# Row attention: the exponential in two instructions by score bank, each with its own sum and signal

## The chip, the cores and the metric

The kernel runs on one core of one Trainium2 chip. The metric is the device time of one execution in microseconds (us), lower is better. The kernel before took 1969.8 us, the median of three runs (1965.45 to 1972.23).

## The reference

A graph network with four residual blocks over 1250 rows of 512 features: a graph attention over edges, a small mixture with low-rank experts, an edge-mean network and, last, a transformer block. The change touches only the attention of that last block. Cut to what matters there:

```
q = (x @ Wq + bq).reshape(B, S, NH, dh)          # B = 1, S = 1250, NH = 8, dh = 64
k = (x @ Wk + bk).reshape(B, S, NH, dh)
v = (x @ Wv + bv).reshape(B, S, NH, dh)
scores = einsum('bqhd,bkhd->bhqk', q, k) / sqrt(dh)
attn = softmax(scores, axis=-1)                  # over all 1250 keys
ctx = einsum('bhqk,bkhd->bqhd', attn, v).reshape(B, S, D)
x = layernorm(x + ctx @ Wo + bo, g1, beta1)      # then a top-1 mixture of 8 experts, a second norm
```

Everything is float32. Where a product needs full precision, both sides are split into a high and a low part and multiplied in three passes.

## The kernel before

All parts of the network follow each other in one program. The stage at issue is `self_attention`, which fills the time from about 1381 us to 1820 us of the profiled span. Each engine has an instruction stream written out by hand; they meet only through semaphores, and no scheduler reorders anything.

**Tiling.** The 1250 queries are cut into 5 chunks of 250, each of two tiles of 125 queries. With 8 heads this gives 16 units a chunk, numbered n = 0 to 15 (head n // 2, tile n % 2), and 80 units in all. One unit is a block of 125 queries by 1250 keys. The text calls it a row of the stage, or a unit.

**One unit, in the order of its data:**

1. `scores(n)` on TensorE, L2812: six matmuls into three PSUM banks (columns 0 to 512, 512 to 1024, 1024 to 1250; two matmuls a bank). There is only one set of these banks, so `scores(n)` waits on `e_ready`, the signal of the exponential of unit n-1. Each bank raises `s_done`.
2. `maximum(n)` on VectorE: one reduction a bank (L2653, tile mmin), then, behind a wait on its own result, a reduction of the three numbers (L2655, tile mbias). It raises `m_ready`.
3. `exponentials(n)` on ScalarE, L2569: one instruction over all 1250 columns from PSUM into `mprob`, with the row sum taken along into `mden`. The trace shows it as two rows: ACTIVATE, and ACTIVATION_READ_ACCUMULATOR, which brings out the sum. It raises `e_ready`.
4. `inverse(n)` on VectorE, L2646: the reciprocal of the sum, tile mrden.
5. GpSimd multiplies the 1250 columns by it, L2540.
6. `turn(n)` on TensorE, L2830: ten transposes in three pieces (4, 4, 2) into three more banks. Each piece waits on `tp_free`, which VectorE raises when it has read the piece of the unit before.
7. `turned_hi(n)` on ScalarE (L2575, tile ptm_hi) and `turned_lo(n)` on VectorE (L2660, tile ptm_lo): high and low part of each piece. The latter raises `tp_free`.
8. `context` on TensorE, L136 to L138: 15 matmuls a unit. `context_hi` (L2580) and `context_lo` (L2666, tile ctx_lo) split its result once in two units.

**Order on each engine.** In step n the engines do work of different units, in this order:

- TensorE: `scores(n)`, then half a `context`, then `turn(n-2)`. Steps 5 and 6 of a chunk also hold the output projection of the chunk before, steps 10 to 13 its gate.
- VectorE: `inverse(n-1)`, in odd steps `context_lo`, then `maximum(n)`, then `turned_lo(n-3)`. Steps 5 to 9 also hold the residual and the norm of the chunk before (`row_sum`, `moments`, `scales`, `centred`, `normal`), steps 12 and 13 its gate and places.
- ScalarE: `exponentials(n)`, in even steps `context_hi`, then `turned_hi(n-2)`.
- GpSimd: the multiplication, and in steps 14 and 15 the indirect DMAs of the chunk before.

The first chunk is unrolled and holds besides, in steps 0 to 2, the values (L136 to L138 over kv_w), and in step 4 the split of the output weights (L2606 on ScalarE, L2774 on VectorE). Chunks 1 to 4 are the turns of a hardware loop. In a loop a wait compares with a register, which an instruction ahead of it computes.

`link` is a helper: it lets a VectorE instruction raise a semaphore and makes VectorE wait for it, so that the next instruction reads a finished result. `CREDITS` gives the semaphores that start above zero.

Of the kernel before, what the change touches and what calls it, by code (L numbers as in the profile page):

```python
# [12 lines left out]
F32 = mybir.dt.float32  # L13
# [5 lines left out]
ALU = mybir.AluOpType  # L19
ACT = mybir.ActivationFunctionType  # L20
AX = mybir.AxisListType

N, D = 1250, 512
P = 125
# [21 lines left out]
SPANS = [(0, 512), (512, 1024), (1024, N)]  # L46
# [46 lines left out]
    return ap.rearrange("p (a n) -> p a n", a=1).broadcast_to([ap.shape[0], t, ap.shape[1]])  # L93


CREDITS = {"at_e_ready": 1, "at_tp_free": 3, "at_c_free": 1, "at_summed": 1, "moe_placed": 1, "moe_scattered": 1}


class Core:


    def __init__(self, nc, stack):
# [6 lines left out]

        self.credits = {name: stack.enter_context(nc.semaphore(name)) for name in CREDITS}  # L110

    def at(self, name, shape, dtype, kb):

        return self.nc.alloc_sbuf_tensor_at(name, shape, dtype, offset=self.bottom + int(kb * 1024))
# [90 lines left out]
def prepare(core, g, w, ln):  # L205
# [89 lines left out]
    with nc.Block() as block:  # L295
        @block.sync
        def _(sp):
            for name, n in CREDITS.items():
                sp.sem_inc(core.credits[name], n)
# [2093 lines left out]
def self_attention(core, g, w):  # L2393
# [6 lines left out]
    nc, at, sem = core.nc, core.at, core.sem  # L2400
    NH, DH = 8, 64
# [6 lines left out]
    prob = at("mprob", [P, 4, N], F32, 92)  # L2408
    xin = at("mha_xin", [P, 2, D], F32, 4)
    S = g.small  # L2410
    low = at("mmin", [P, 2, 4], F32, S)
    bias, den, rden = (at(n, [P, 4], F32, S + .125 + i / 16) for i, n in enumerate(("mbias", "mden", "mrden")))

    rows, rows_t = at("slot_rows", [P, 2, ROW], F32, 188), at("gate_xt", [128, 2, KT, P], F32, 128)
    g1, beta1 = at("moe_g1", [P, D], F32, 204.25), at("moe_beta1", [P, D], F32, 10)
# [28 lines left out]
    s_done, m_ready, e_ready = sem("at_s_done"), sem("at_m_ready"), sem("at_e_ready")  # L2444
    r_ready, p_ready = sem("at_r_ready"), sem("at_p_ready")
# [9 lines left out]
    SUBS = 2 * NH  # L2455
    score = core.psum[0:P, 0:3, :].rearrange("p b n -> p (b n)")
# [18 lines left out]
    def chunks(eng, chunk, counts):  # L2475

        chunk(0, range(SUBS), lambda j: j >= 0)
        with eng.Fori(1, NC) as c:
            for tick, per in counts:
                tick.enter(c - 1, per)  # L2480
            chunk(c, range(SUBS), lambda j: True)
            for tick, per in counts:
                tick.leave(NC - 1)
        chunk(NC, range(LAST), lambda j: j < 0)
# [4 lines left out]
    with nc.Block() as block:  # L2489
# [73 lines left out]
        @block.scalar  # L2563
        def _(act):
            sub, tp, ctx = Tick(), Tick(), Tick()

            def exponentials(n):
                act.wait_ge(m_ready, sub.step())
                nc.scalar.activation(prob[:, n % 4, :], score[:, 0:N], ACT.Exp, bias=bias[:, n % 4:n % 4 + 1],  # L2569
                                     scale=-1.0, accum_out=den[:, n % 4:n % 4 + 1]).then_inc(e_ready, 1)  # L2570

            def turned_hi(n):
                for q, (j0, j1) in enumerate(PIECES):
                    act.wait_ge(tp_done, tp.step())
                    nc.scalar.activation(pt_part(n, 0, j0, j1), piece(q), ACT.Copy).then_inc(tp_hi, 1)  # L2575

            def context_hi(hh):
                rows_, k, _ = place(2 * hh)
                act.wait_ge(c_done, ctx.step())
                nc.scalar.activation(ctx_hi[rows_, k, :], ctx_bank[rows_, 0:CH], ACT.Copy).then_inc(c_hi, 1)  # L2580

            def weights_1(experts):
                for e in experts:
                    act.wait_ge(w1_in[e], 16)
                    nc.scalar.activation(g.w1_hi[:, e, :, :], g.raw1[:, e, :, :], ACT.Copy).then_inc(w_hi, 1)

            def weights_2(experts):
                for e in experts:
                    act.wait_ge(w2_in[e], 16)
                    nc.scalar.activation(g.w2_hi[:, e, :, :], g.raw2[:, e, :, :], ACT.Copy).then_inc(w_hi, 1)  # L2590

            def chunk(c, steps_, live):
                for n in steps_:
                    if live(n):
                        exponentials(n)
                    if n < len(VALUES) and isinstance(c, int) and c == 0:
                        for t in VALUES[n]:
                            act.wait_ge(v_summed, t + 1)
                            nc.scalar.activation(g.v_hi[:, t, :], vsum[:, t % 2, :], ACT.Copy).then_inc(v_top, 1)
                    if n % 2 == 0 and live(n - 6):  # L2600
                        context_hi((n - 6) % SUBS // 2)
                    if live(n - 2):
                        turned_hi((n - 2) % SUBS)
                    if n == 4 and isinstance(c, int) and c == 0:
                        act.wait_ge(g.wo_in, 16)
                        nc.scalar.activation(wo_hi[:], raw[:], ACT.Copy).then_inc(wo_h, 1)  # L2606
                    if n == 6 and not live(0):
                        weights_1(range(NE))
                        weights_2(SECOND[:4])
                    if n in (10, 11) and live(-1):  # L2610
                        s = n - 10
                        act.wait_ge(gt_done, 2 * (c - 1) + s + 1)
                        nc.scalar.activation(rows_t[:, s, :, :], gate_bank[:, 0:KT * P].rearrange("p (k n) -> p k n", k=KT),
                                             ACT.Copy).then_inc(gt_out, 1)
                if not live(0):
                    weights_2(SECOND[4:])

            chunks(act, chunk, ((sub, SUBS), (tp, 3 * SUBS), (ctx, NH)))
            mix.scalar(act)

        @block.vector
        def _(dve):
            link = core.link.on(dve)
            spans, tp, ctx, exps = Tick(), Tick(), Tick(), Tick()
# [17 lines left out]
                nc.vector.tensor_tensor(g.v_lo[:, t, :], vsum[:, t % 2, :], f32(g.v_hi[:, t, :]), ALU.subtract).then_inc(v_low, 1)  # L2642

            def inverse(n):
                dve.wait_ge(e_ready, 1 + exps.step())
                nc.vector.reciprocal(rden[:, n % 4:n % 4 + 1], den[:, n % 4:n % 4 + 1]).then_inc(r_ready, 1)  # L2646

            def maximum(n):

# [105 lines left out]
            def chunk(c, steps_, live):  # L2755
                for n in steps_:
                    if live(n - 1):
                        inverse((n - 1) % SUBS)
# [38 lines left out]
                    for i in range(1, EARLY):  # L2797
                        lower_2(i)

            chunks(dve, chunk, ((spans, 3 * SUBS), (exps, SUBS), (tp, 3 * SUBS), (ctx, NH), (link, SUBS + 2 + 13 + 5 + 6)))  # L2800
            mix.vector(dve, lambda: [lower_2(i) for i in range(EARLY, NE)])

        @block.tensor
        def _(pe):
            exps, sub, tp, ctx = Tick(), Tick(), Tick(), Tick()

            def scores(n):
                cols = place(n)[2]
                pe.wait_ge(e_ready, exps.step())
                for a, b in SPANS:  # L2810
                    for half in range(2):
                        last = nc.tensor.matmul(score[:, a:b], qs[:, half, n // 2, cols], g.k_stack[:, n // 2, a:b],  # L2812
                                                start=half == 0, stop=half == 1)
                    last.then_inc(s_done, 1)
# [91 lines left out]
                    if n == 13 and live(-1):  # L2906
                        counts(c)

            chunks(pe, chunk, ((exps, SUBS), (sub, SUBS), (tp, 3 * SUBS), (ctx, NH)))
            mix.tensor(pe)  # L2910


# [331 lines left out]
```

## Time and profile before

| | |
|---|---|
| median of three runs | 1969.8 us (1965.45 to 1972.23) |
| the profiled execution | 1970.24 us, of which 1968.6 us is the span of the trace |
| granted TensorE clock, mean over the span | 0.958 |
| TensorE busy | 1780.5 us (90%) |
| VectorE busy | 1318.9 us (67%) |
| ScalarE busy | 907.6 us (46%) |
| GpSimd busy | 588.9 us (30%) |
| exponentials, L2569 | 80 of 1304 ns, 104.3 us, and 80 reads of the sum of 192 ns |
| scores, L2812 | 480 matmuls |

A busy share is a mean over stages that have different limits; what a change of one stage is worth is read from that stage. Matmuls are pipelined and their ends are modelled, so neighbouring matmuls overlap in the trace, and a busy TensorE is not one at its peak. An instruction on VectorE or ScalarE can start a little before the one ahead has ended, too, so the distance from start to start is often less than a duration. An idle time stands in brackets behind an instruction, with what ended it. Where one engine waits for several semaphores, the trace names the one that came last by its own reckoning.

### The profile page before, as it was taken

Reading aid. Unit: us, or ns where it says so; the run is one execution under the profiler, and the core shown is the slowest. Engines: PE = TensorE matmul, PEld = TensorE weight load, DVE = VectorE, ACT = ScalarE, POOL = GpSimd, SP = SyncE. Lnnn points to the kernel's source line nnn. Section 1 sums busy time; section 2 is a strip of 40 time slices with the busy share of each in tenths; the row PEclk is TensorE's granted clock in tenths of the full one; section 3 lists DMA queues with packets and bytes.
Section 4 is the critical chain, followed back from the end, with each engine's and each line's share of the span. In section 5 each row is a group of like instructions: output and inputs, shape, how many; then the busy total and the mean of one; then the engine's idle time right before and its main releaser. Section 6 shows DMA issues by size and latency. Waiting matters only on the chain. (4 is left out here: it accounts for less than half of the span.)

```text
span 1968.6 us, 31926 instructions
## 1 busy us (share of the span) xinstructions
PE 1780.5 (90%) x10958; PEld 1548.7 (79%) x10958; DVE 1318.9 (67%) x2945; ACT 907.6 (46%) x1652; POOL 588.9 (30%) x531
## 2 busy tenths in 40 slices
PE   7998969899999999898677999999889999999496
PEld 5776769888888888777565998988788888888385
DVE  5444336688888888377763455655578787887676
ACT  4332236677777776222230223424365555555421
POOL 0000030365555652011100220222244544454234
PEclk9999979999999999999888999999999999999698
DMA  6752496677787774665356673125011211113532
GB/s 237 209 186 88 140 291 198 192 206 204 199 203 201 204 200 137 159 155 150 94 128 151 134 188 97 43 84 175 22 22 22 64 31 31 31 31 103 174 120 86
DMA packets 183532, 265.14 MB, mean 135 GB/s; under 512 B 55852, under 2 KB 102443, under 8 KB 181109
## 3 DMA queue, kind: packets, MB, share of 16 engines
q1 hardware_dynamic: 117839, 169.58, 29.7%
q0 software_dynamic: 49920, 62.94, 12.0%
q10 hardware_dynamic: 15640, 30.90, 6.3%
q8 instruction: 76, 1.25, 0.3%
q14 instruction: 57, 0.47, 0.1%
HBM read 198.55 MB, written 85.86 MB: 144 GB/s over the span
## 5 line engine op out<-in xcount | busy, mean ns | idle before, releaser
L1063 POOL DMA_INDIRECT edge_rows<-xn_store,edge_index x200 | 243.5, 1218 | 254.1 <-PE psum L138 104.8
L2540 POOL TENSOR_TENSOR mprob<-mprob,mrden 125x1250 f32<-125x1250 f32 x80 | 181.6, 2272 | 220.5 <-DVE mrden L2646 220.0
L2569 ACT ACTIVATE mprob<-psum,mbias 125x1250 f32<-125x1250 f32 x80 | 104.3, 1304 | 153.6 <-DVE mbias L2655 153.6
L1279 DVE TENSOR_TENSOR edge_xt_lo<-psum,edge_xt_hi 128x500 fp32r<-128x500 f32 x200 | 134.7, 675 | 52.0 <-ACT edge_xt_hi L1156 52.0
L2653 DVE TENSOR_REDUCE mmin<-psum 125x1 f32<-125x512 f32 (+1 forms) x240 | 126.9, 584 | 47.8 <-PE psum L2812 47.6
L1156 ACT ACTIVATE edge_xt_hi<-psum 128x500 fp32r<-128x500 f32 x200 | 117.5, 589 | 87.5 <-PE psum L1442 87.5
L2830 PE MATMUL psum<-ident,mprob 125*125 125x125 f32 x800 | 117.9, 292 | 18.8 <-DVE ptm_lo L2660 9.5
L2830 PEld LDWEIGHTS psum<-ident,mprob 125*125 125x125 f32 x800 | 100.3, 191 | 36.5 <-DVE ptm_lo L2660 20.5
L2660 DVE TENSOR_TENSOR ptm_lo<-psum,ptm_hi 125x500 fp32r<-125x500 f32 (+1 forms) x240 | 126.3, 582 | 2.0 <-ACT ptm_hi L2575 2.0
L1442 PE MATMUL psum<-ident,edge_rows 125*128 125x125 f32 x800 | 119.5, 272 | 3.7 <-DVE edge_xt_lo L1279 2.0
L1308 DVE TENSOR_TENSOR edge_rows_lo<-edge_rows,edge_rows_hi 125x1024 fp32r<-125x1024 f32 x100 | 121.2, 1212 | 0.0
L136 PE MATMUL psum<-ptm_hi,v_hi 125*128 125x250 f32 x400 | 114.2, 285 | 4.8 <-DVE ctx_lo L2666 4.8
L2575 ACT ACTIVATE ptm_hi<-psum 125x500 fp32r<-125x500 f32 (+1 forms) x240 | 109.9, 516 | 14.4 <-PE psum L2830 13.5
L136 PE MATMUL psum<-xt_hi,fc_hi 128*128 128x250 f32 x320 | 95.5, 299 | 23.0 <-DVE hid_lo L2074 19.8
L2812 PE MATMUL psum<-k_stack,q_chunk 128*125 128x512 f32 (+1 forms) x480 | 112.8, 371 | 3.0 <-PEq L126 2.9
L137 PE MATMUL psum<-ptm_lo,v_hi 125*128 125x250 f32 x400 | 112.6, 282 | 0.0
L138 PE MATMUL psum<-ptm_hi,v_lo 125*128 125x250 f32 x400 | 112.2, 280 | 0.0
L136 PE MATMUL psum<-edge_xt_hi,t_row 128*100 128x500 f32 x200 | 110.1, 551 | 0.0
L1442 PEld LDWEIGHTS psum<-ident,edge_rows 125*128 125x128 f32 x800 | 96.0, 142 | 17.1 <-DVE edge_xt_lo L1279 2.2
L136 PE MATMUL psum<-xt_hi,qk_hi 128*128 128x250 f32 x320 | 91.9, 287 | 16.0 <-DVE t_part L1269 16.0
L1162 ACT ACTIVATE edge_rows_hi<-edge_rows 125x1024 fp32r<-125x1024 f32 x100 | 105.2, 1053 | 0.0
L1143 ACT ACTIVATE t_part<-psum,t_cols 128x250 fp32r<-128x250 f32 x80 | 59.3, 752 | 89.6 <-PE psum L138 62.8
(519 smaller groups left out, 5415.4 us busy)
## 6 DMA issues: line engine op xcount, KB each, us to landing
slots_in<-blank_rows ACTq DMA_DIRECT2D x20, 1026.0 KB, 7.9
t_store<-t_part SPq DMA_DIRECT2D x20, 1000.0 KB, 5.2
t_row<-t_store SPq DMA_DIRECT2D x47, 400.0 KB, 6.6
y_store<-y_rows SPq DMA_DIRECT2D x50, 200.0 KB
q_chunk<-q_store SPq DMA_DIRECT2D x40, 250.0 KB, 5.3
y_tile<-y_store SPq DMA_DIRECT2D x10, 896.0 KB
edge_attr<-in_attr SPq DMA_DIRECT2D x50, 112.0 KB
moe_xg<-slots_in SPq DMA_DIRECT2D x17, 256.5 KB, 3.6
```

Of the source, the lines that this page charges most:

```text
L136: nc.tensor.matmul(out, lh, rh, start=start, stop=False)
L137: nc.tensor.matmul(out, lh, rl, start=False, stop=False)
L1063: nc.gpsimd.indirect_dma_start(xe[t % RING][:, s, :], None, g.xn_store, bass.IndirectOffsetOnAxis(ap=index[t % RING][:, s, 0:1], axis=0)). ...
L1156: nc.scalar.activation(xt_hi[:, k, :], x_bank(KT * t + k), ACT.Copy).then_inc(x_top, 1)
L1279: nc.vector.tensor_tensor(xt_lo[:, k, :], x_bank(KT * t + k), f32(xt_hi[:, k, :]), ALU.subtract).then_inc(x_low, 1)
L1308: nc.vector.tensor_tensor(xe_lo[t % RING][:, halves(q), :], xe[t % RING][:, halves(q), :], f32(xe_hi[t % 3][:, halves(q), :]), ALU.subtrac ...
L1442: last = nc.tensor.transpose(x_bank(n)[:, s * P:(s + 1) * P], xe[t % RING][:, s, k * 128:(k + 1) * 128], g.ident[0:P, 0:P])
L2540: nc.gpsimd.tensor_tensor(prob[:, n % 4, :], prob[:, n % 4, :], rden[:, n % 4:n % 4 + 1].broadcast_to([P, N]), ALU.mult).then_inc(p_ready, 1)
L2653: last = nc.vector.tensor_reduce(low[:, s, q:q + 1], score[:, a:b], AX.X, ALU.min)
L2660: nc.vector.tensor_tensor(pt_part(n, 1, j0, j1), piece(q), f32(pt_part(n, 0, j0, j1)), ALU.subtract).then_inc(tp_free, 1)
L2812: last = nc.tensor.matmul(score[:, a:b], qs[:, half, n // 2, cols], g.k_stack[:, n // 2, a:b], start=half == 0, stop=half == 1)
L2830: last = nc.tensor.transpose(piece(q)[:, j - j0, :], prob[:, n % 4, j * P:(j + 1) * P], g.ident[0:P, 0:P])
```

## The change

The exponential of a unit becomes two instructions on ScalarE: one over columns 0 to 512 (the first score bank), one over columns 512 to 1250 (the other two). Each writes its own sum and raises `e_ready` by one. `scores(n)` waits for the first signal ahead of bank 0 and for the second ahead of bank 1, and bank 2 follows without a wait. `inverse(n)` waits for both, adds the two sums, waits for the result through `link`, and takes the reciprocal.

```diff
-CREDITS = {"at_e_ready": 1, "at_tp_free": 3, ...
+CREDITS = {"at_e_ready": 2, "at_tp_free": 3, ...
...
-    bias, den, rden = (at(n, [P, 4], F32, S + .125 + i / 16) for i, n in enumerate(("mbias", "mden", "mrden")))
+    bias, rden = (at(n, [P, 4], F32, S + .125 + i / 16) for i, n in enumerate(("mbias", "mrden")))
+    den = at("mden", [P, 2, 4], F32, S + .25)
+    EXPS = (slice(0, SPANS[0][1]), slice(SPANS[0][1], N))
...
             def exponentials(n):
                 act.wait_ge(m_ready, sub.step())
-                nc.scalar.activation(prob[:, n % 4, :], score[:, 0:N], ACT.Exp, bias=bias[:, n % 4:n % 4 + 1],
-                                     scale=-1.0, accum_out=den[:, n % 4:n % 4 + 1]).then_inc(e_ready, 1)
+                for i, cols in enumerate(EXPS):
+                    nc.scalar.activation(prob[:, n % 4, cols], score[:, cols], ACT.Exp, bias=bias[:, n % 4:n % 4 + 1],
+                                         scale=-1.0, accum_out=den[:, i, n % 4:n % 4 + 1]).then_inc(e_ready, 1)
...
             def inverse(n):
-                dve.wait_ge(e_ready, 1 + exps.step())
-                nc.vector.reciprocal(rden[:, n % 4:n % 4 + 1], den[:, n % 4:n % 4 + 1]).then_inc(r_ready, 1)
+                dve.wait_ge(e_ready, 2 + exps.step(2))
+                own = slice(n % 4, n % 4 + 1)
+                link(nc.vector.tensor_tensor(rden[:, own], den[:, 0, own], den[:, 1, own], ALU.add))
+                nc.vector.reciprocal(rden[:, own], rden[:, own]).then_inc(r_ready, 1)
...
             def scores(n):
                 cols = place(n)[2]
-                pe.wait_ge(e_ready, exps.step())
-                for a, b in SPANS:
+                before = exps.step(2)
+                for q, (a, b) in enumerate(SPANS):
+                    if q < 2:
+                        pe.wait_ge(e_ready, before - 1 + q)
                     for half in range(2):
                         last = nc.tensor.matmul(score[:, a:b], qs[:, half, n // 2, cols], g.k_stack[:, n // 2, a:b],
                                                 start=half == 0, stop=half == 1)
```

The counts that the hardware loop keeps (`chunks(...)` on VectorE and TensorE) follow: two signals of `exps` a unit, and one more `link` a unit.

On VectorE, from `centred` in step 8 of the loop to the first reduction of step 9 (slot_rows is written by `centred`, mrden by `inverse`, ctx_lo by `context_lo`, mmin by `maximum`; REGISTER_ALU computes the number that a wait compares with), before:

```order
L2693 SCALAR_TENSOR_TENSOR slot_rows<-mha_xin,ln_mean_var,moe_g_19413 125x512 x2
L2645 REGISTER_ALU
L2646 RECIPROCAL mrden<-mden 125x1
L2665 REGISTER_ALU
L2666 TENSOR_TENSOR ctx_lo<-psum,ctx_hi 64x250
L2652 REGISTER_ALU
L2653 TENSOR_REDUCE mmin<-psum 125x1
```

and now:

```order
L2698 SCALAR_TENSOR_TENSOR slot_rows<-mha_xin,ln_mean_var,moe_g_19413 125x512 x2
L2648 REGISTER_ALU
L2650 TENSOR_TENSOR mrden<-mden 125x1
L88 REGISTER_ALU
L2651 RECIPROCAL mrden<-mrden 125x1
L2670 REGISTER_ALU
L2671 TENSOR_TENSOR ctx_lo<-psum,ctx_hi 64x250
L2657 REGISTER_ALU
L2658 TENSOR_REDUCE mmin<-psum 125x1
```

An addition and a wait stand ahead of the reciprocal; nothing else has changed places.

On TensorE, from the last piece of a `turn` to the end of the scores of the next step (MATMUL psum<-ident,mprob is a transpose, psum<-k_stack,q_chunk a score matmul), before:

```order
L2830 MATMUL psum<-ident,mprob 125x125 [waits at_tp_free]
L2830 MATMUL psum<-ident,mprob 125x125
L2809 REGISTER_ALU
L2812 MATMUL psum<-k_stack,q_chunk 125x512 [waits at_e_ready]
L2812 MATMUL psum<-k_stack,q_chunk 125x512 x3
L2812 MATMUL psum<-k_stack,q_chunk 125x226 x2
```

and now:

```order
L2837 MATMUL psum<-ident,mprob 125x125 [waits at_tp_free]
L2837 MATMUL psum<-ident,mprob 125x125
L2817 REGISTER_ALU
L2819 MATMUL psum<-k_stack,q_chunk 125x512 [waits at_e_ready]
L2819 MATMUL psum<-k_stack,q_chunk 125x512
L2817 REGISTER_ALU
L2819 MATMUL psum<-k_stack,q_chunk 125x512 [waits at_e_ready]
L2819 MATMUL psum<-k_stack,q_chunk 125x512
L2819 MATMUL psum<-k_stack,q_chunk 125x226 x2
```

The scores still stand behind the whole `turn`; a second wait has come between their first and second bank.

## Rows read from the trace of the kernel before

**Rows 1.** Stretches, an ordinary and a full one: length, busy us by engine, clock

```profile
1440.00:1480.00 40.00, 39.02 (x283) 35.72 (x282) 32.38 (x77) 26.04 (x51) 20.56 (x10) 1.00 0.16 34
1516.00:1534.00 18.00, 16.91 (x119) 14.98 (x117) 17.35 (x46) 10.53 (x20) 9.08 (x4) 1.00 0.30 62
```

**Rows 2.** Timeline, TensorE, first chunk and loop: start us, us, engine, line, operation

```profile
1443.51 1.41 PE L2830 MATMUL psum<-ident,mprob 125*125 125x125 f32 x10
...
1523.82 1.31 PEld L2830 LDWEIGHTS psum<-ident,mprob 125*125 125x125 f32 x10 [0.57 <-DVE ptm_lo L2660]
...
1565.56 1.50 PE L2830 MATMUL psum<-ident,mprob 125*125 125x125 f32 x10
1566.79 1.22 PEld L2812 LDWEIGHTS psum<-k_stack,q_chunk 128*125 128x125 f32 x6
...
1571.25 1.24 PEld L2812 LDWEIGHTS psum<-k_stack,q_chunk 128*125 128x125 f32 x6
```

**Rows 3.** Timeline, ScalarE, exponentials of steps 7 and 2

```profile
1519.67 0.19 ACT L2569 ACTIVATION_READ_ACCUMULATOR mprob<-psum,mbias 125x1 f32 x1
...
1569.38 1.30 ACT L2569 ACTIVATE mprob<-psum,mbias 125x1250 f32<-125x1250 f32 x1 [1.30 <-DVE mbias L2655]
1570.58 0.19 ACT L2569 ACTIVATION_READ_ACCUMULATOR mprob<-psum,mbias 125x1 f32 x1
```

**Rows 4.** Timeline, VectorE, ordinary steps; in brackets the idle time ahead

```profile
1494.20 1.59 DVE L2653 TENSOR_REDUCE mmin<-psum 125x1 f32<-125x512 f32 x3 [0.56 <-PE psum L2812]
...
1502.26 0.42 DVE L2666 TENSOR_TENSOR ctx_lo<-psum,ctx_hi 64x250 fp32r<-64x250 f32 x1 [0.23 <-ACT ctx_hi L2580]
1503.05 1.59 DVE L2653 TENSOR_REDUCE mmin<-psum 125x1 f32<-125x512 f32 x3 [0.37 <-PE psum L2812]
...
1563.11 1.59 DVE L2653 TENSOR_REDUCE mmin<-psum 125x1 f32<-125x512 f32 x3 [1.30 <-PE psum L2812]
...
1570.80 0.16 DVE L2646 RECIPROCAL mrden<-mden 125x1 f32<-125x1 f32 x1
```

**Rows 5.** Timeline, VectorE, full steps 7 and 8

```profile
1520.43 0.16 DVE L2385 TENSOR_TENSOR ln_h<-ln_r 125x2 f32<-125x2 f32 x1
1520.62 0.16 DVE L2386 TENSOR_TENSOR ln_h<-ln_h,ln_ve 125x2 f32<-125x2 f32 x1
...
1521.31 0.16 DVE L2646 RECIPROCAL mrden<-mden 125x1 f32<-125x1 f32 x1
1521.41 1.59 DVE L2653 TENSOR_REDUCE mmin<-psum 125x1 f32<-125x512 f32 x3
```

**Rows 6.** Chain of waits, second chunk: start us, us, engine, tile, line

```profile
1525.92 0.15 DVE mrden L2646
...
1533.54 1.50 PE psum L2830 x10
```

**Rows 7.** Groups by line and shape, ScalarE: busy us, mean ns, idle before

```profile
L2569 ACT ACTIVATE mprob<-psum,mbias 125x1250 f32<-125x1250 f32 x80 | 104.3, 1304 | 153.6 <-DVE mbias L2655 153.6
L1168 ACT ACTIVATE prob<-psum,nb 100x500 f32<-100x500 f32 x50 | 33.9, 678 | 19.1 <-DVE nb L1284 19.1
```

**Rows 8.** Timeline, ScalarE, an exponential with sum in the graph attention

```profile
599.69 0.68 ACT L1168 ACTIVATE prob<-psum,nb 100x500 f32<-100x500 f32 x1 [0.34 <-DVE nb L1284]
600.27 0.20 ACT L1168 ACTIVATION_READ_ACCUMULATOR prob<-psum,nb 100x1 f32 x1
600.36 0.28 ACT L1170 ACTIVATE corr<-max_bound,nb 100x1 f32<-100x1 f32 x1
```

**Rows 9.** Chain of waits, first chunk

```profile
1415.66 0.69 DVE v_lo L2642
...
1423.86 1.39 ACT mprob L2569 x2
...
1426.64 1.81 ACT wo_hi L2606
1428.48 2.29 DVE wo_lo L2774
```

More of the change, by code:

```diff
@@ L93, in bc @@
     return ap.rearrange("p (a n) -> p a n", a=1).broadcast_to([ap.shape[0], t, ap.shape[1]])
-CREDITS = {"at_e_ready": 1, "at_tp_free": 3, "at_c_free": 1, "at_summed": 1, "moe_placed": 1, "moe_scattered": 1}
+CREDITS = {"at_e_ready": 2, "at_tp_free": 3, "at_c_free": 1, "at_summed": 1, "moe_placed": 1, "moe_scattered": 1}
 class Core:
@@ L2798, in chunk @@
                         lower_2(i)
-            chunks(dve, chunk, ((spans, 3 * SUBS), (exps, SUBS), (tp, 3 * SUBS), (ctx, NH), (link, SUBS + 2 + 13 + 5 + 6)))
+            chunks(dve, chunk, ((spans, 3 * SUBS), (exps, 2 * SUBS), (tp, 3 * SUBS), (ctx, NH), (link, 2 * SUBS + 2 + 13 + 5 + 6)))
             mix.vector(dve, lambda: [lower_2(i) for i in range(EARLY, NE)])
@@ L2907, in chunk @@
                         counts(c)
-            chunks(pe, chunk, ((exps, SUBS), (sub, SUBS), (tp, 3 * SUBS), (ctx, NH)))
+            chunks(pe, chunk, ((exps, 2 * SUBS), (sub, SUBS), (tp, 3 * SUBS), (ctx, NH)))
             mix.tensor(pe)
```

## The prediction

> **What bounds the kernel now.** I read the page first: TensorE is busy 90% of the span, but that is a mean over all stages, so I went to the stage of the change by stretches [rows 1]. In ordinary steps TensorE is busy 39.02 of 40 us, VectorE 32.38. In the stretch 1516 to 1534 it turns over: VectorE is busy 17.35 of 18 us. So there are two kinds of steps, and a cost on VectorE or ScalarE is judged by the kind in which it falls.
>
> Then the timelines, to see what each engine waits for. An ordinary step of the loop is 4.46 us long (1566.79 to 1571.25 [rows 2]). Its cycle is: `turn` on TensorE, the first score bank, VectorE's reductions, its first ptm_lo, the next `turn`. The exponential isn't in this cycle. The sum of step 2 is out at 1570.58 + 0.19 = 1570.77 [rows 3]; the weights of the next scores load at 1571.25 [rows 2], right behind a `turn` that takes 1.50 us in each of these steps. TensorE takes its work in order, so the scores can't start earlier however early the exponential signals: there are 0.48 us of slack ahead of the wait that the change splits.
>
> VectorE in ordinary steps has time to spare ahead of `maximum`. I counted the 80 starts of mmin: in 10 the wait for TensorE is 0.36 to 0.40 us (the row with 0.37), in 11 it is 0.51 to 0.56, in 4 it is 0.94, in 26 over 1.0 (the row with 1.30) [rows 4], and in the other 29 there is none. Of these, 24 are steps 7, 8, 9, 10, 13 and 14 of the four loop turns (step 8 stands in [rows 5]), five are in the first chunk. The chain of waits goes through VectorE there, by name through the reciprocal [rows 6], and only goes back to TensorE with the `turn` at 1533.54.
>
> **The change part by part.**
>
> *Earlier first signal.* Worth the time by which the scores wait for the exponential. No start of the scores in the stage has such a wait; gain 0. Its bounds: nothing, and 0.05 us in each of the 51 steps with a wait ahead of mmin, if the start of the weight load hangs on the signal and not on the `turn`: 2.6 us.
>
> *Second exponential.* Two exponentials with bias and sum from PSUM stand in the trace, 1304 ns for 1250 columns and 678 ns for 500 [rows 7]: 626 / 750 = 0.835 ns a column and 261 ns fixed. So 512 columns take 0.69 us and 738 take 0.88. Start to start, the read of the sum follows 0.10 us before the exponential's end [rows 3], and the next instruction with a bias starts 0.09 us behind the start of the read [rows 8]. The pair then reads its last sum at 0.59 + 0.09 + 0.78 = 1.46 us behind its start, now at 1.20: the exponential comes 0.25 us later. If the second must wait for the read to end, 0.35; if nothing overlaps at all (0.69 + 0.19 + 0.88 + 0.19 = 1.95 against 1.39) 0.56. Below, the gain side, is excluded: the same columns are read with one more fixed part. I take 0.25, the value with a neighbour of the same form.
>
> Who waits for it? ptm_hi, the next on ScalarE, is read by VectorE only behind the next unit's `maximum`, so it is covered. `inverse` starts 0.03 us behind the read (1570.80 [rows 4]), and in the odd steps ctx_hi, then ctx_lo, then `maximum`. That path has 0.37 us in its tightest 10 steps, so 0.25 is covered with 0.12 to spare. In the full steps the exponential is long done: the sum is out at 1519.86 [rows 3], the reciprocal comes at 1521.31 [rows 5]. GpSimd's product comes 0.45 us later (0.25 + 0.20), and its `turn` is two steps away. The scores' wait keeps 0.48 - 0.25 = 0.23 us even by the last signal, which is now asked for only ahead of bank 1, half a microsecond on. Once it shows: in the first chunk, exponential, ptm_hi, wo_hi and wo_lo stand in one chain [rows 9]. Cost 0.25 us.
>
> *The addition.* A small VectorE instruction behind a wait on the one ahead comes 0.19 us after it (1520.43 to 1520.62), which I round up to 0.20, one without such a wait 0.10 (reciprocal 1521.31, mmin 1521.41) [rows 5]. The addition is followed by a `link`, so it costs that. In ordinary steps it lies in the spare time: in the tight ones VectorE waits 0.23 us between the reciprocal and ctx_lo for ctx_hi [rows 4], and the addition fits into that. In the full steps it lies on the path: 6 steps x 4 turns x 0.20 = 4.8 us. Behind it wait `maximum`, mbias, the exponential and ptm_lo, and through ptm_lo the `turn` of TensorE, which waits there already (0.57 us at 1523.82 [rows 2]), so nothing takes the delay up. In the first chunk two reciprocals stand on the chain, one behind v_lo, one behind wo_lo [rows 9]: 0.4 us. Bounds: 0.10 each, if the wait costs nothing more, makes 2.6 us for these 26; 0.30 each, if the computed number of the wait is late too, 7.8.
>
> The Trainium skill (VectorE: DVE Perf Modes, "The DRAIN you can't avoid") says that the semaphore between chained VectorE instructions costs nothing extra. The trace disagrees for these small ones: 0.19 with, 0.10 without [rows 5]. By the page the addition would add 2.6 us instead of 5.2.
>
> *Second wait of the scores.* One register instruction and one wait between bank 0 and bank 1. Bank 0's matmuls take about 0.5 us and TensorE's queue runs ahead under them; 0. For the other side: a `turn` takes 1.50 us in the loop, 1.41 in the unrolled chunk [rows 2], where its three waits compare with constants, so 0.03 us a wait; over 64 units at most 1.9 us, and no more than half of it on the path.
>
> *The end.* The last reciprocal is covered by GpSimd's DMAs ahead of its product.
>
> **Sum.** 0 + 0.25 + 5.2 + 0 = 5.5 us. Against the profiled execution of 1970.24 that is 1975.7; this execution lies 0.4 us above the median of 1969.8, so I expect a median of 1975.3, 0.28% more. About 0.3% (5.9 us) is what a measurement of this kernel can tell from no change, so this is a small loss just at that edge.
>
> **The rivals.**
>
> *A, the exponential's cover is too thin (slower).* It decides from 0.37 us on. For it: the margin is only 0.12 us and rests on a fit from two shapes. Against: the read of a sum overlaps its neighbours in both places where it stands. At 0.56 us the 10 tight steps lose 0.18 each (1.8), the 11 next ones, whose reciprocal and ctx_lo lie closer, 0.07 (0.8), the first chunk 0.3 more: 5.5 + 2.9 = 8.4 us, 1978.2; with the second wait of the scores on top 1979 to 1980.
>
> *B, the addition is cheaper (no change).* The page's rule, or part of the full steps' delay taken up where VectorE waits anyway: 2.6 + 0.25 or less, 1972.5. For it: unlinked neighbours at 0.10. Against: the linked pair at 0.19, and VectorE is busy 17.35 of 18 us from 1516 to 1534 [rows 1].
>
> *C, the scores do start earlier (faster).* The change then does what it says in every ordinary step: the first bank comes sooner, and VectorE's 0.37 to 1.06 us of waiting shrink. For it: that wait is real, and it is for the scores. Against: `turn` stands between, and TensorE has no gap ahead of the scores. If the start moved by 0.15 us in 51 steps, -7.7 + 5.5 = -2.2 us, 1967.6; to be faster beyond 0.3% it would take 0.22.
>
> *D, the first signal is of no use and every cost is covered.* It would need the full steps not to be VectorE's; the chain excludes that, and I put it with B.
>
> **How the numbers follow.** Forecast 0.55, A 0.23, B 0.15, C 0.07. The forecast itself spreads from 1972.5 to 1978.5 with the medians of three runs (7 us apart before), and 0.4 of it lies above 1975.7: 0.22. Of A nearly all is slower (0.21), of B nothing. Slower 0.43. C gives faster 0.04, and the scatter of the medians 0.02 more: 0.06. The rest, 0.51, is no change. The range reaches from 1969 (most of B) to 1981 (A with its bounds).
>
> **What would show it.** Right: the reads of the sum double to 160; exponentials of about 690 and 880 ns, 1.46 us from the start of the first to the last read; in steps 7 to 10, 13 and 14 mmin starts 0.3 us behind the start of the addition, where it was 0.1 behind the reciprocal's, and each of these steps is 0.20 us longer; the ordinary step still 4.46 us with mmin's wait down from 0.37 to about 0.12; the stage 5 to 6 us longer and everything else as before. Wrong: an ordinary step that has changed its length (longer: A, shorter: C), a wait of the scores for mprob, or full steps that are no longer.

## The result, and the profile after

The change takes 1976.07 us (median of 20 runs) against 1972.48 us for the kernel before (20 runs). The quotient of the two medians is 1.0018. The ratio used here is 1.0023, 95% interval 1.0012 to 1.0034; it is taken over all runs but one slow run of the change (2062.72 us at a granted clock of 0.823). It is a small, real loss, inside the 0.3% that the prediction called no change. The profiled execution took 1979.71 us (span 1978.1), before 1970.24 (1968.6).

Of these 9.5 us of span only 6.1 belong to the stage. From the first mmin to the last it went from 422.13 us (1383.36 to 1805.49) to 428.21 us (1388.13 to 1816.34). The rest is scatter from elsewhere: the first mmin comes anywhere between 1383.04 and 1391.60 us in the traces of this case, in kernels that do the same work up to there. So I compare kernels by the time from the mmin of step 7 in the first chunk to the last one, "the stage time" below: **364.49 us before, 370.23 us with the change, +5.74**. Ahead of it the change loses another 0.34 us. That part can't be read to a few tenths, since the granted clock falls in it: before, it is 0.84 from 1383 to 1390 us and 0.76 from 1418 to 1425. In experiment 1, where it is 1.00 from 1390 to 1432, the same part is 2.8 us shorter.

The exponential first, from the timeline of ScalarE with the change, step 4 (start, duration; in brackets the idle time ahead). It answers to [rows 3].

```profile
1505.52 0.69 ACT L2572 ACTIVATE mprob<-psum,mbias 125x512 f32<-125x512 f32 x1 [1.57 <-DVE mbias L2660]
1506.11 0.19 ACT L2572 ACTIVATION_READ_ACCUMULATOR mprob<-psum,mbias 125x1 f32 x1
1506.20 0.87 ACT L2572 ACTIVATE mprob<-psum,mbias 125x738 f32<-125x738 f32 x1
1506.96 0.20 ACT L2572 ACTIVATION_READ_ACCUMULATOR mprob<-psum,mbias 125x1 f32 x1
1507.18 0.38 ACT L2583 ACTIVATE ctx_hi<-psum 64x250 fp32r<-64x250 f32 x1
```

The last read starts 1506.96 - 1505.52 = 1.44 us behind the first exponential; it was 1.20, so the sum is 0.24 us later. Now VectorE with the change, steps 4 and 5, which answers to [rows 4]:

```profile
1503.71 1.59 DVE L2658 TENSOR_REDUCE mmin<-psum 125x1 f32<-125x512 f32 x3 [0.59 <-PE psum L2819]
...
1507.19 0.16 DVE L2650 TENSOR_TENSOR mrden<-mden 125x1 f32<-125x1 f32 x1 [0.21 <-ACT mprob L2572]
1507.39 0.16 DVE L2651 RECIPROCAL mrden<-mrden 125x1 f32<-125x1 f32 x1
1507.59 0.42 DVE L2671 TENSOR_TENSOR ctx_lo<-psum,ctx_hi 64x250 fp32r<-64x250 f32 x1
1508.14 1.59 DVE L2658 TENSOR_REDUCE mmin<-psum 125x1 f32<-125x512 f32 x3
```

The step is 1508.14 - 1503.71 = 4.43 us long, to the hundredth what it was (1498.62 to 1503.05). There is a new wait of 0.21 us for the exponential, and the gap ahead of mmin shrank: from 0.37 us to 1508.14 - (1507.59 + 0.42) = 0.13, so little that no idle time is given in brackets. In steps 1 to 4 the wait for the scores shrank to 0.15, 0.62, 0.28 and 0.59 us, each by 0.25 to 0.44. Slack is used up in every ordinary step, and none of it shows in the length.

In the full steps there was no slack. Step 8 with the change, answering to [rows 5]:

```profile
1521.07 0.16 DVE L2387 SCALAR_TENSOR_TENSOR ln_r<-ln_h,ln_r 125x2 f32<-125x2 f32 x1
1521.35 0.16 DVE L2650 TENSOR_TENSOR mrden<-mden 125x1 f32<-125x1 f32 x1
1521.55 0.16 DVE L2651 RECIPROCAL mrden<-mrden 125x1 f32<-125x1 f32 x1
1521.64 0.41 DVE L2671 TENSOR_TENSOR ctx_lo<-psum,ctx_hi 64x250 fp32r<-64x250 f32 x1
1521.98 1.57 DVE L2658 TENSOR_REDUCE mmin<-psum 125x1 f32<-125x512 f32 x3
...
1526.61 0.16 DVE L2650 TENSOR_TENSOR mrden<-mden 125x1 f32<-125x1 f32 x1
1526.81 0.16 DVE L2651 RECIPROCAL mrden<-mrden 125x1 f32<-125x1 f32 x1
1526.90 1.29 DVE L2658 TENSOR_REDUCE mmin<-psum 125x1 f32<-125x512 f32 x2
```

Addition to reciprocal is 0.20 us (1526.61 to 1526.81), reciprocal to mmin 0.09. The time from mmin to mmin is 4.92 us, before 4.73. Averaged over the four loop turns, steps 7, 8, 9, 10 and 13 grew by 0.19, 0.19, 0.20, 0.21 and 0.10 us, and step 14, where undisturbed, from 5.51 to 5.70.

One thing was in no part of the prediction. The addition takes 0.16 us in 77 of 80 units and up to 1.73 in the other three. VectorE in step 2 of loop turn 3, then GpSimd at the same time, with the change (slots_in is the target of an indirect DMA):

```profile
1659.18 1.59 DVE L2665 TENSOR_TENSOR ptm_lo<-psum,ptm_hi 125x500 fp32r<-125x500 f32 x3
1660.94 1.60 DVE L2650 TENSOR_TENSOR mrden<-mden 125x1 f32<-125x1 f32 x1 [0.17 <-ACT mprob L2572]
1662.57 0.16 DVE L2651 RECIPROCAL mrden<-mrden 125x1 f32<-125x1 f32 x1
1662.67 1.59 DVE L2658 TENSOR_REDUCE mmin<-psum 125x1 f32<-125x512 f32 x3
```

```profile
1659.93 0.20 POOL L2560 TENSOR_TENSOR passed<-zeros 125x2 f32<-125x2 f32 x1 [4.50 <-DMA slots_in<-slot_rows,moe_place]
1660.25 2.27 POOL L2542 TENSOR_TENSOR mprob<-mprob,mrden 125x1250 f32<-125x1250 f32 x1
1662.81 2.27 POOL L2542 TENSOR_TENSOR mprob<-mprob,mrden 125x1250 f32<-125x1250 f32 x1 [0.29 <-DVE mrden L2651]
```

The product ends at 1660.25 + 2.27 = 1662.52, the addition at 1662.54. An addition of two columns lasts until GpSimd is done. Normally a product is over long before the next addition; here GpSimd came late, behind its DMAs of steps 14 and 15. Step 2 is 0.74 us longer in loop turn 3 and 0.88 in turn 4 (addition at 1744.90, 1.73 us). In turn 2 (1577.75, 0.62 us) the wait for the scores hides it.

**Where the 5.74 us are:** 4.11 in the 24 full steps, 1.62 in the two held additions, about 0 in everything else. In the 4.11 a disturbance has nearly cancelled. One step 14 of each of these two executions is longer at a lower granted clock: 6.35 us in turn 3 before, 6.37 in turn 1 with the change. Without both the full steps give 4.11 + 0.84 - 0.67 = 4.28. The windows of that step, the kernel before and then the change (length, busy us, granted clock, DMA):

```profile
1712.00:1719.00 7.00, 6.28 (x38) 6.05 (x38) 5.01 (x18) 2.73 (x5) 2.27 (x1) 0.76 0.00 0
```

```profile
1554.00:1561.00 7.00, 6.57 (x41) 6.39 (x42) 5.18 (x18) 2.97 (x7) 2.34 (x2) 0.76 0.01 2
```

The same stretches of the other kernel have a clock of 1.00. In the 7 us ahead of them the clock was 1.00 too, with TensorE busy 6.97 us before and 6.52 with the change.

### The profile page after: what moved, and what is told of

It reads as the page before. It is cut to its first block and busy times, and to the rows that moved or that the text cites. A ratio compares the mean times of both kernels' runs of the same rounds, so it can differ in the third digit from the quotient of the medians.

```text
span 1978.1 us, 32350 instructions
## 1 busy us (share of the span) xinstructions
PE 1787.8 (90%) x10958; PEld 1553.2 (79%) x10958; DVE 1335.5 (68%) x3025; ACT 921.4 (47%) x1812; POOL 590.3 (30%) x531
## 5 line engine op out<-in xcount | busy, mean ns | idle before, releaser
L2572 ACT ACTIVATE mprob<-psum,mbias 125x512 f32<-125x512 f32 (+1 forms) x160 | 123.7, 778 | 149.9 <-DVE mbias L2660 149.9
```

The source lines that it names most:

```text
L2572: nc.scalar.activation(prob[:, n % 4, cols], score[:, cols], ACT.Exp, bias=bias[:, n % 4:n % 4 + 1], scale=-1.0, accum_out=den[:, i, n % 4 ...
```

## The experiments

The theory at the start: the loss is the addition in the full steps, and the split exponential costs and brings nothing. Its rivals: the exponential's cover is too thin, and the early signal does bring something that the addition hides. Ratios are against the kernel before, run on the same chip.

**1. The change without the addition.** The reciprocal takes the first sum only; the second is left out.

```diff
-link(nc.vector.tensor_tensor(rden[:, own], den[:, 0, own], den[:, 1, own], ALU.add))
-nc.vector.reciprocal(rden[:, own], rden[:, own]).then_inc(r_ready, 1)
+nc.vector.reciprocal(rden[:, own], den[:, 0, own]).then_inc(r_ready, 1)
```

> Leaves out the second sum: the reciprocal is taken of the first alone, without addition and link; both exponentials and both waits of the scores stay. From the first mmin to the last the stage took 422.1 us before and 428.2 us with the change. Theory 'addition' (24 full steps x 0.19 us, plus an addition held up by GpSimd's product, 1.6 us): falls back to 422.3 to 422.8, full steps as before (4.73, 5.15, 4.59 us), whole kernel 1970 to 1972 (ratio to before about 1.000). Rival 'exponential' (its 0.25 us more are what costs): stays near 427 to 428, ratio about 1.0025.

1971.93 against 1971.62 us, ratio 1.0003 (0.9987 to 1.0019); the stage time is 364.54 us, 0.05 from the kernel before, and no step from there on differs by more than 0.04. (Both traces have one slow step 14, of 6.35 us.) From the first mmin on the stage took 419.39 us, less than the 422.3 to 422.8 that were expected; the difference is the 2.8 us ahead of step 7 told above. In step 8 reciprocal and mmin stand 0.11 us apart, with nothing ahead of them:

```profile
1525.64 0.16 DVE L2650 RECIPROCAL mrden<-mden 125x1 f32<-125x1 f32 x1
1525.75 1.59 DVE L2657 TENSOR_REDUCE mmin<-psum 125x1 f32<-125x512 f32 x3
```

So split exponentials, two signals and two waits together are worth nothing either way from step 7 on.

**2. The addition alone.** The kernel before, with a column of zeros added to its sum.

```diff
-nc.vector.reciprocal(rden[:, n % 4:n % 4 + 1], den[:, n % 4:n % 4 + 1]).then_inc(r_ready, 1)
+link(nc.vector.tensor_tensor(rden[:, own], den[:, own], none[:, 0:1], ALU.add))
+nc.vector.reciprocal(rden[:, own], rden[:, own]).then_inc(r_ready, 1)
```

> One exponential over all columns as before, but VectorE adds a column of zeros to its sum behind a link, so the addition alone. Theory 'addition': stage 422.1 + 24 x 0.19 + 0.4 = 427.1 us, and up to 1.6 more where the addition falls into one of GpSimd's products; steps 8, 9, 10 are 4.92, 5.34, 4.80; ratio 1.0025. Rival 'exponential': stage about 422.5, ratio 1.000.

1980.19 us, ratio 1.0044 (1.0025 to 1.0062). The stage time is 370.23 us, the same as the change's: the full steps give 4.3 us without the clock's part, as there, and the held additions 1.4. The addition carries the whole loss. It is held here too, as VectorE's timeline and then GpSimd's show:

```profile
1660.89 2.22 DVE L2649 TENSOR_TENSOR mrden<-mden,mnone 125x1 f32<-125x1 f32 x1
```

```profile
1660.83 2.27 POOL L2541 TENSOR_TENSOR mprob<-mprob,mrden 125x1250 f32<-125x1250 f32 x1
```

The product lasts until 1663.10, the addition until 1663.11.

**3. One wait.** The change, with both signals awaited ahead of bank 0.

```diff
-if q < 2:
-    pe.wait_ge(e_ready, before - 1 + q)
+if q == 0:
+    pe.wait_ge(e_ready, before)
```

> The change, with the scores waiting for both exponentials ahead of bank 0, so the early signal is unused. Theory (the scores stand behind the turn and have slack): stage 428 us within 1 us, ordinary steps still 4.46 and 4.42, no wait of the scores for mprob. Rival (the early signal hides a cost): ordinary steps longer by 0.05 us or more, stage over 430.

One execution, 1980.82 us. The ordinary steps are 4.42 to 4.46 us as in the change: giving the early signal up costs nothing. The stage time of 373.25 us would mislead: three of its steps 14 take 6.48, 6.53 and 7.59 us instead of 5.70, the last at a clock of 0.59 from 1805 to 1813. These are worth 0.78 + 0.83 + 1.89 = 3.5 us, the one such step of the change 0.67. The difference, 2.8, is nearly all of the 3.0 between the two.

**4. A reduction in place of the addition.** The two sums lie side by side and one instruction with a single input adds them.

```diff
-den = at("mden", [P, 2, 4], F32, S + .25)
+den = at("mden", [P, 4, 2], F32, S + .25)
...
-link(nc.vector.tensor_tensor(rden[:, own], den[:, 0, own], den[:, 1, own], ALU.add))
+link(nc.vector.tensor_reduce(rden[:, own], den[:, n % 4, :], AX.X, ALU.add))
```

> The change, with the two sums side by side and added by a reduction, which reads one tensor instead of two. Theory 'held by GpSimd': in three steps of the change's profile the addition of 0.16 us took 0.62, 1.60 and 1.73, until GpSimd's product ended; with one input none of the 80 is over 0.2 us, the stage 1.5 us shorter than the change's, 426.5 us. Rival (something else stretches a small VectorE instruction there): reductions of 0.6 us and more in steps 1 and 2 of the turns remain.

One execution, 1976.71 us. The durations of this line (shortest/median/longest of 80, ns) in the change, then here:

```profile
L2650 DVE TENSOR_TENSOR mrden<-mden x80: 148/159/1726, 1401.2 to 1819.8; 125x1 f32<-125x1 f32 x80
```

```profile
L2650 DVE TENSOR_REDUCE mrden<-mden x80: 147/155/158, 1399.7 to 1816.2; 125x1 f32<-125x2 f32 x80
```

And GpSimd and then VectorE at the place where the addition was held:

```profile
1658.18 4.50 POOL L2542 TENSOR_TENSOR mprob<-mprob,mrden 125x1250 f32<-125x1250 f32 x2
```

```profile
1658.93 0.16 DVE L2650 TENSOR_REDUCE mrden<-mden 125x1 f32<-125x2 f32 x1 [0.17 <-ACT mprob L2572]
```

GpSimd is late here as well: two products follow each other without a gap. The reduction starts inside the first and takes 0.16 us. This holds in every trace. In the five that have the addition (the change, experiments 2, 3 and 5, and the second run of 6), 13 additions start inside a product of GpSimd, and each ends with it, to 0.02 us. In the four with the reduction 11 start inside one, and none takes more than 0.16 us. The stage time is 367.88 us, 2.35 less than the change's: 1.62 are the held additions, 0.67 is the clock, which leaves all steps 14 alone here (5.69 to 5.70 us). The full steps cost as much as with the addition: 3.38, or 4.22 without the slow step of the kernel before.

> The changed kernel with the sums added by a reduction of one tensor, as seen once before, now timed. Theory (24 x 0.19 + 0.4 us remain, the additions held up by GpSimd's product are gone): ratio to before 1.001 to 1.003, 1 to 2 us less than the change in its own two medians; no reduction over 0.2 us. Rival: as slow as the change or slower, 1.0023 to 1.005.

Timed, the same kernel takes 1978.79 us, ratio 1.0030 (1.0014 to 1.0046), stage time 367.84. No reduction is held in this trace either (145 to 158 ns). The traces show 1.6 us saved in the stage, twice; the medians don't show it, and the intervals of the two ratios overlap. That the kernel as a whole is faster with the reduction is not shown.

**5. Three exponentials, one a bank.** Three sums; the third is left out of the addition.

```diff
-EXPS = (slice(0, SPANS[0][1]), slice(SPANS[0][1], N))
+EXPS = tuple(slice(a, b) for a, b in SPANS)
```

> The change with three exponentials, one a bank, the sum of the third left out of the addition (still two addends). Another 0.25 us from the exponential's start to its last sum. Theory: the tight ordinary steps (5 of each turn, 9 and 13 of the first chunk), whose wait ahead of mmin is gone already with two, now each lose 0.2 us; steps 1 lose 0.1 (0.15 left); the others (0.28 and more left) nothing; stage 1.5 to 2.5 us over the change. Rival (there is cover left): no ordinary step longer than 4.47.

One execution, 1982.66 us. Steps 4 and 5 on VectorE:

```profile
1504.97 1.59 DVE L2660 TENSOR_REDUCE mmin<-psum 125x1 f32<-125x512 f32 x3 [0.34 <-PE psum L2821]
...
1508.69 0.16 DVE L2652 TENSOR_TENSOR mrden<-mden 125x1 f32<-125x1 f32 x1 [0.45 <-ACT mprob L2572]
...
1509.54 1.59 DVE L2660 TENSOR_REDUCE mmin<-psum 125x1 f32<-125x512 f32 x3
```

The wait for the exponential grew from 0.21 to 0.45 us, and step 5 to 4.57. Steps 1 and 5 of each turn and steps 9 and 13 of the first chunk lose 0.11 to 0.17 us; those that still wait for the scores (0.34 here) lose nothing. The sum comes another 0.24 us later, and step 5 takes 0.14 of it up in length: the change had left 0.10 us of margin in that step. In a turn most of what step 5 loses comes back at once: step 6, which waits 1.40 us for the scores, takes 6.61 to 6.66 us where it took 6.77 to 6.79. The stage time of 371.78 us is 1.55 over the change's, inside the 1.5 to 2.5 that were expected, but by luck: the tight steps give about 0.8 of it, an addition of 2.24 us in step 2 of turn 2, with the steps behind it, about 1.3 more than the held additions of the change, and no step 14 is slow here (0.67 less).

**6. The cycle of an ordinary step.** The prediction said that it runs through VectorE's first ptm_lo. If so, doing that piece ahead of `maximum` shortens the step. First on the kernel before, in every step:

```diff
+if live(n - 3):
+    turned_lo((n - 3) % SUBS, 0, 1)   # piece 0, ahead of maximum(n)
...
-turned_lo((n - 3) % SUBS)
+turned_lo((n - 3) % SUBS, 1, 3)       # pieces 1 and 2, behind it
```

> The kernel before, with one edit on VectorE: the first of the three ptm_lo pieces is done ahead of maximum, in the time in which VectorE waits for the scores, and the other two behind it. Theory (the ordinary step is the cycle turn, first score bank, maximum, first ptm_lo, so the turn is what the early signal can't get past): the turn no longer waits, and the ordinary step falls from 4.46 us to 4.15 to 4.25, where the exponential's single signal becomes the limit (0.76 to the first bank, 1.8 for the reductions, 1.5 for the exponential and its sum, 0.1); 51 steps x 0.25, the stage 410 us instead of 422, ratio 0.993 to 0.995. Rival (TensorE itself is the limit): step stays 4.4 or more, ratio 1.000.

1970.8 against 1972.58 us, ratio 0.9999 (0.9983 to 1.0016): the expected gain did not come. The stage time fell by 2.65 us, to 361.84, and the ordinary steps go from 4.45 to 4.31 in some and to 4.56 or 4.84 in the odd ones. VectorE has new waits:

```profile
1490.32 1.00 DVE L2660 TENSOR_TENSOR ptm_lo<-psum,ptm_hi 125x500 fp32r<-125x500 f32 x2
1491.83 0.16 DVE L2646 RECIPROCAL mrden<-mden 125x1 f32<-125x1 f32 x1 [0.52 <-ACT mprob L2569]
1492.32 0.68 DVE L2660 TENSOR_TENSOR ptm_lo<-psum,ptm_hi 125x500 fp32r<-125x500 f32 x1 [0.32 <-ACT ptm_hi L2575]
```

ScalarE in the same step:

```profile
1491.61 0.19 ACT L2569 ACTIVATION_READ_ACCUMULATOR mprob<-psum,mbias 125x1 f32 x1
1491.70 1.33 ACT L2575 ACTIVATE ptm_hi<-psum 125x500 fp32r<-125x500 f32 x3
```

A second cycle lies close behind the first: maximum, exponential, the first ptm_hi behind it on ScalarE, the first ptm_lo, the next maximum. The reciprocal is not in it: it is done at 1491.99, and VectorE waits on until 1492.32 for ptm_hi. No mmin of an ordinary step waits for the scores any more. On this order the split exponential ought to cost its full price. The same edit on the change:

> The same edit on the changed kernel. Theory: with the turn out of the way the early signal is worth something; the ordinary step is TensorE's own work, 4.05 to 4.15 us, 0.05 to 0.1 us less than in the same edit on the kernel before, against 24 x 0.19 us and GpSimd's hold on the addition in the full steps: both about equal, ratio 0.993 to 0.997. Rival (the early signal is worthless here too): ordinary step equal to or longer than in the edit on the kernel before, and 5 us or more behind it in all.

1984.13 us, ratio 1.0068 (1.0048 to 1.0089), stage time 376.92. The steps are some 0.24 us longer than in the run above (4.55 and 4.80 for 4.31 and 4.56), which is what the second exponential and its read take:

```profile
1493.17 0.16 DVE L2650 TENSOR_TENSOR mrden<-mden 125x1 f32<-125x1 f32 x1 [0.76 <-ACT mprob L2572]
1493.36 0.16 DVE L2651 RECIPROCAL mrden<-mrden 125x1 f32<-125x1 f32 x1
1493.65 0.68 DVE L2665 TENSOR_TENSOR ptm_lo<-psum,ptm_hi 125x500 fp32r<-125x500 f32 x1
```

The wait for the exponential is 0.76 us where it was 0.52. ScalarE, and then the weight loads of the scores:

```profile
1492.93 0.20 ACT L2572 ACTIVATION_READ_ACCUMULATOR mprob<-psum,mbias 125x1 f32 x1
1493.03 1.33 ACT L2578 ACTIVATE ptm_hi<-psum 125x500 fp32r<-125x500 f32 x3
```

```profile
1492.79 0.30 PEld L2821 LDWEIGHTS psum<-k_stack,q_chunk 128*125 128x125 f32 x2
1493.18 0.36 PEld L2821 LDWEIGHTS psum<-k_stack,q_chunk 128*125 128x125 f32 x2
```

The first ptm_lo starts 0.62 us behind ptm_hi, as in the run above (1492.32 - 1491.70). The addition's 0.20 us fits into the wait for ptm_hi and costs nothing in these steps. And the early signal is used here: the weights of the first score bank load at 1492.79, 0.34 us ahead of the end of the last read of a sum (1493.13), those of the second bank 0.05 behind it. In the run above the first bank's came 0.05 us behind the end of the only read. But nobody waits for these scores: mmin (1494.24) stands behind ptm_lo. So the expected gain of 0.05 to 0.1 us a step did not come. With the reduction of experiment 4 it was no better:

> The changed kernel with the sums added by a reduction of one tensor, and the first ptm_lo piece ahead of maximum. Theory: as the same edit on the changed kernel, without the additions that GpSimd holds up: 1 to 2 us less than that, ratio 0.992 to 0.996. Rival: no difference between the two.

1986.83 us, ratio 1.0082 (1.0060 to 1.0105), stage time 378.06, where 1 to 2 us less than above were expected. Two of its steps 14 are slow (7.55 and 6.28 us for 5.66) and one of the run above (6.50); without them the stage times are 375.55 and 376.08.

**7. The first piece early in even steps only.** The odd steps hold ctx_lo as well and are the long ones above, so they keep their order.

```diff
+if live(n - 3) and n % 2 == 0:
+    turned_lo((n - 3) % SUBS, 0, 1)
...
-turned_lo((n - 3) % SUBS)
+turned_lo((n - 3) % SUBS, 0 if n % 2 else 1, 3)
```

> The kernel before with the first ptm_lo piece ahead of maximum in even steps only, where VectorE waits over 1.0 us for the scores; odd steps keep the old order. With the piece first in all steps the pair of steps became 4.31 + 4.84 (or 4.31 + 4.56) where it was 4.46 + 4.46, because VectorE then waits for the exponential ahead of the piece. Theory (only the odd steps had no room): pair of 4.31 + 4.46, 0.15 us for 26 even steps, stage 4 us shorter than 422, ratio 0.998. Rival (the gain of an even step is paid back by the odd one behind it, since both hang on VectorE's and ScalarE's chain): pair still 8.9 us, ratio 1.000.

On the kernel before: **1964.64 us (1959.08 to 1967.34) against 1971.78, ratio 0.9964 (0.9947 to 0.9982)**. It is faster than both kernels. Two steps on VectorE:

```profile
1488.81 0.68 DVE L2660 TENSOR_TENSOR ptm_lo<-psum,ptm_hi 125x500 fp32r<-125x500 f32 x1 [0.41 <-ACT ptm_hi L2575]
1489.46 1.59 DVE L2653 TENSOR_REDUCE mmin<-psum 125x1 f32<-125x512 f32 x3
...
1493.48 1.59 DVE L2653 TENSOR_REDUCE mmin<-psum 125x1 f32<-125x512 f32 x3
...
1497.91 1.59 DVE L2653 TENSOR_REDUCE mmin<-psum 125x1 f32<-125x512 f32 x3
```

The odd step takes 4.02 us (1489.46 to 1493.48), the even one 4.43 as before. In the turns steps 1 and 2 together take 8.55 us for 8.92, steps 3 and 4 8.45 for 8.89, where 0.15 us less a pair was expected. In steps 1 to 5 of the turns mmin now waits 0.13 us at most (0.36 to 1.07 before). The stage time is 356.03 us, 8.5 less, of which 0.84 is the slow step 14 of the kernel before. With split exponentials and the reduction the same order gives:

> The same order on the changed kernel with the reduction as addition. Theory: the exponential's 0.25 us and the addition's 0.19 now lie on the path of every even step: pair 0.2 to 0.4 us longer than in the same edit on the kernel before, stage 430 or more, ratio 1.003 to 1.008. Rival (the early signal helps here): pair shorter than 8.9, ratio 1.000.

1974.73 us, ratio 1.0014 (0.9996 to 1.0032), stage time 364.46. That is 8.4 us more, 0.7 of it a slow step 14: the change takes back what the order brings. In the odd steps the early signal does let the scores start early. An odd step, on ScalarE, TensorE and VectorE in turn:

```profile
1492.16 0.20 ACT L2572 ACTIVATION_READ_ACCUMULATOR mprob<-psum,mbias 125x1 f32 x1
1492.02 1.23 PEld L2821 LDWEIGHTS psum<-k_stack,q_chunk 128*125 128x125 f32 x6
1493.25 1.59 DVE L2658 TENSOR_REDUCE mmin<-psum 125x1 f32<-125x512 f32 x3
```

The weights of the scores load 0.34 us ahead of the end of the last read (1492.36). It brings nothing: mmin stands behind the reduction (1492.40, after a wait of 0.76 us for the last sum), the reciprocal and ctx_lo (1492.80).

## Why the prediction was right

**The sum.** Its profiled form said 5.5 us; the stage shows 6.1. Its median said 1975.3 us, the runs 1976.07; in ratio 0.28% against 0.23%. That the absolute times lie so close is partly luck: 1975.3 was counted from 1969.8, and the median before is 1972.48 over 20 runs.

**Earlier first signal, 0.** Right: experiment 3 removes it and no ordinary step changes, and experiment 1 keeps it and gains nothing. With the change the weights of the scores load 0.20 us or more behind the last read's end in every step from step 7 of the first chunk on (0.23 was forecast), before 0.44 or more.

**Second exponential, 0.25 once.** Right in size (0.24 us later, against 0.25 from the fit), in cover and in margin: 0.12 us were to be left of 0.37 in a tight step, 0.13 stand in the trace and experiment 5 finds 0.10. Whether it costs its 0.25 in the first chunk is not shown by itself. The addition's 0.20 fits into the old wait for ctx_hi (0.23, [rows 4]), as forecast.

**The addition, 4.8 + 0.4.** Right in kind (experiments 1 and 2) and close in size. The full steps give 3.2 us in steps 7 to 10, 0.4 in step 13 (half of the forecast; it grew by 0.16 in three turns, and in turn 1, where it was longer before, it shrank by 0.06) and 0.8 in step 14: 4.3 without the clock's part, where 4.8 were forecast. In the first chunk exponential and additions together give 0.34, where 0.65 were: its steps 1 and 5 grow by 0.18 and 0.27, and steps 4 and 6, which wait for the scores, give 0.06 and 0.05 back. With the clock falling there, this is no measurement of the 0.65. The Trainium skill's sentence that the semaphore costs nothing extra (VectorE: DVE Perf Modes, "The DRAIN you can't avoid") does not hold for these small instructions: 0.20 us with the wait, 0.09 without. Rival B is out by that.

**What was missed, 1.62 us.** The prediction priced the addition as an instruction of 0.16 us wherever it stands. It did not ask what GpSimd does meanwhile. The Trainium skill has the rule (SBUF — State Buffer, "Who interferes with whom"): a VectorE instruction with two inputs in SBUF and a GpSimd instruction that reads SBUF share a read port, and the second to start waits for the whole of the first; a reduction never does. The trace agrees on both: the addition ends with the product, to 0.02 us, while the reduction inside a product takes 0.16. It is the rule against this change that should have been weighed. How much it costs is chance: in the five traces with the addition the held ones take 0.41 to 2.24 us, depending on how late GpSimd is. That the forecast came near all the same is luck, since the full steps (0.5) and the first chunk (0.3) cost less than forecast and the clock took 0.2 less from the change.

**Second wait of the scores, 0.** Right, within the 0.05 us by which the stage of experiment 1 differs.

**Rivals.** A (cover too thin) did not happen, but it was near: 0.10 us more on the exponential would begin it, and experiment 5 shows it, though in the turns step 6 then gives most of step 5's loss back. C (scores start earlier) is out by experiments 1 and 3.

**The cycle.** "Turn, first score bank, reductions, first ptm_lo, next turn" was true but not the whole: taking ptm_lo out of it in every step gains little in the stage (2.65 us, 0.84 of it the clock) and nothing that the medians show (experiment 6), since the cycle through the exponential and ptm_hi is nearly as long. Only where both have room is there a gain (experiment 7). That steps 8 and 10 grow by some 0.55 us in that order, and 9 and 11 shrink by as much, is the way of counting from mmin to mmin: the piece now stands ahead of mmin in the even steps. Steps 8 and 9 together take 9.84 us for 9.88, steps 10 and 11 9.41 for 9.42.

**Open.** The two traces differ by 6.1 us in the stage, the medians by 3.6; the interval of the ratio, 2.4 to 6.7 us, holds both. Experiment 2's ratio is above the change's at an equal stage time, and the 1.6 us of experiment 4 are in no median. Time outside the stage differs by more than that from run to run, and the runs don't settle it.

## What to carry over

An earlier signal is worth the wait of its reader, not the length of the work that it cuts: look first at what stands ahead of the reader in its own queue, and then whether anybody waits for the reader (in experiments 6 and 7 the scores did start earlier, and nothing waited for them). A reduction that is cut in two needs its parts joined, and that joining lands on the engine that is full, once a unit. When an instruction with two SBUF inputs is added to VectorE, look in the trace for what GpSimd runs beside it, in the steps where GpSimd is late too; a one-input form avoids the question.

## What the runs showed of the hardware that was not expected

- A VectorE addition of 125x1 elements takes 0.16 us, and 0.41 to 2.24 us, until the product's end, if it starts inside GpSimd's product of 2.27 us (13 of 13). A reduction of 125x2 takes 0.15 to 0.16 us there (11 of 11).
- An exponential with bias and sum takes 0.69 us for 512 columns, 0.87 for 738 and 0.44 for 226. A read of the sum between two of them costs 0.19 us of its own row, but the next starts 0.09 us behind its start.
- The granted clock falls for a few us at step 14, to a mean of 0.76 over 7 us or 0.59 over 8, in one to three of the four loop turns of some executions and in none of others (experiments 4 and 5). It costs 0.6 to 1.9 us each time, and moves stage times between runs by as much as the effects studied here.
